# A fused transformer kernel: the high part of the rotated queries and keys is copied on GpSimd instead of ScalarE, and the order of the work is fitted anew

## The reference

```python
x = x + attn_a(layernorm(x), ...)
x = x + ffn(layernorm(x), w_gate, w_up, w_down)
x = x + attn_b(layernorm(x), Wqkv, Wout, bout)
x = x + ffn(layernorm(x), w_gate, w_up, w_down)

# in attn_b
re = te * cos - to * sin
ro = te * sin + to * cos
q_rot, k_rot = rotate(q), rotate(k)
num = exp(q_rot @ k_rot.T * scale)                  # rotated queries and keys
den = sum(exp(q @ k.T * scale), keys)               # not rotated, over all keys
attn = where(causal, num / den, 0)
y = attn @ v @ Wout + bout
```

## Time and profile before

| | before |
|---|---|
| median of 3 runs | 2028.87 us (2023.63 to 2030.54) |
| the profiled execution: its own time | 2020.54 us |
| its span, first to last instruction | 2018.3 us |
| TensorE busy | 1802.5 us, 89% |
| VectorE busy | 1429.3 us, 71% |
| ScalarE busy | 1429.0 us, 71% |
| GpSimd busy | 803.8 us, 40% |
| granted TensorE clock, mean | 0.946 |

### The profile page before, as it was taken

One profiled execution on the slowest core, in us unless ns is written; L12 is line 12 of the kernel. 1 busy time (PEld: TensorE's weight loads), 2 busy tenths in 40 slices (PEclk: granted clock), 3 DMA queues, 4 the chain that ended last, 5 costly groups with the idle time before them and its releaser, 6 DMA issues.

```text
span 2018.3 us, 63373 instructions
## 1 busy us (share of the span) xinstructions
PE 1802.5 (89%) x25221; PEld 1140.4 (57%) x25221; DVE 1429.3 (71%) x2978; ACT 1429.0 (71%) x3591; POOL 803.8 (40%) x1140
## 2 busy tenths in 40 slices
PE   5577999999899999999899999999999999998775
PEld 3363556566565655656565565656565565655444
DVE  6374768677686867768786877778786777865634
ACT  2227787786868778786877869686877868687590
POOL 0423343533434343443434344343435434344431
PEclk9687999999998999999999999999999999999897
DMA  5223344352524435253534525253443525243321
GB/s 155 64 56 90 87 129 98 100 119 77 136 63 131 91 101 124 78 130 69 137 78 116 122 76 127 72 134 70 138 100 89 127 75 139 61 125 90 73 68 36
DMA packets 129204, 199.51 MB, mean 99 GB/s; under 512 B 26720, under 2 KB 60512, under 8 KB 128880
## 3 DMA queue, kind: packets, MB, share of 16 engines
q1 hardware_dynamic: 128912, 195.44, 38.1%
HBM read 67.87 MB, written 51.52 MB: 59 GB/s over the span
## 4 chain that ended last, share of the span: by engine, by line
PE 47%; ACT 19%; DVE 16%; DMA 7%; issue 5%; SPq 3%; POOL 2%; POOLq 0%; DVEq 0%; ACTq 0%
PE psum L1120 14%; ACT psum L1236 7%; PE psum L1138 7%; ACT probs_B L1226 6%; PE psum L1150 5%; DMA xn<-o_scr_B 4%; PE psum L1017 4%; ACT probs_A L1219 3%; PE psum L1084 3%; PE psum L1094 3%; PE psum L1053 3%; DVE top L1410 2%; SPq L634 2%; PE psum L883 2%; PE psum L1038 2%
## 5 line engine op out<-in xcount | busy, mean ns | idle before, releaser
L1236 ACT ACTIVATE psum<-psum 128x512 f32<-128x512 f32 x1024 | 605.2, 598 | 164.4 <-PE psum L1017 163.5
L1659 POOL TENSOR_TENSOR h<-tmp,h 128x512 f16<-128x512 f32 x192 | 227.6, 1185 | 423.1 <-DVE h L1540 412.7
L1226 ACT ACTIVATE probs_B<-psum 128x512 f32<-128x512 f32 x640 | 334.5, 630 | 34.8 <-PE psum L1038 32.6
L1676 POOL TENSOR_SCALAR_AFFINE_SELECT probs_B<-probs_B 128x256 f32<-128x256 f32 x512 | 201.4, 421 | 117.7 <-ACT probs_B L1226 117.6
L1017 PE MATMUL psum<-pack_b 48*128 48x512 f16 x1024 | 176.9, 394 | 39.6 <-DMA pack_b<-src_b 20.3
L1120 PE MATMUL psum<-xT,w_u 128*128 128x256 f16 x1536 | 210.9, 278 | 1.2
L1120 PE MATMUL psum<-xT,w_g 128*128 128x256 f16 x1536 | 208.8, 280 | 3.1 <-ACT xT L1254 2.6
L1236 ACT ACTIVATION_READ_ACCUMULATOR psum<-psum 128x1 f32 x1024 | 204.2, 199 | 0.0
L1138 PE MATMUL psum<-w_d,h 128*128 128x256 bf16 x1536 | 194.7, 273 | 5.6 <-POOL h L1659 5.6
L1642 POOL TENSOR_TENSOR veps<-mv,eps 128x4 f32<-128x4 f32 x64 | 12.9, 202 | 426.0 <-DVE mv L1490 426.0
L1523 DVE SCALAR_TENSOR_TENSOR tmp<-tmp,psum 128x512 f32<-128x512 f32 x192 | 128.1, 680 | 69.9 <-ACT tmp L1265 69.3
(11 more groups left out here) (150 smaller groups left out, 3229.3 us busy)
## 6 DMA issues: line engine op xcount, KB each, us to landing
pack_b<-src_b SPq DMA_DIRECT2D x768, 64.0 KB, 2.4
pack_a<-src_a SPq DMA_DIRECT2D x384, 64.0 KB, 2.3
x<-in_L_attn_a_x_dram SPq DMA_DIRECT2D x32, 512.0 KB, 4.3
o_scr_A<-o_raw SPq DMA_DIRECT2D x64, 256.0 KB, 4.7
o_scr_B<-o_raw SPq DMA_DIRECT2D x64, 256.0 KB, 2.8
xn<-o_scr_A SPq DMA_DIRECT2D x32, 256.0 KB
rden_on<-r_scr_A SPq DMA_DIRECT2D x32, 256.0 KB
x_scr<-x SPq DMA_DIRECT2D x16, 512.0 KB, 3.1
```

Of the source, the lines that this page charges most:

```text
L1226: act.activation(probs["B"][:, i, :], score_bank("NP", n // 2, q, n % 2)[:, :], ACT.Exp, scale=SM_SCALE / W_SCALE ** 2)\
L1236: act.activation(bank[:, :], bank[:, :], ACT.Exp, scale=SM_SCALE / W_SCALE ** 2, accum_out=den[:, 0, j, 2 * tile + e, t:t + 1]).then_inc(d ...
L1659: pool.tensor_tensor(h[1][:, i % 2, :], tmp[:, i % 2, :], h[0][:, i % 2, :], ALU.subtract)\
L1676: ins = pool.affine_select(a, a, [[0, 2], [1, P]], ALU.is_ge, 0.0, base=0, channel_multiplier=-1)
```

## The change

The copy of the high part moves from ScalarE to GpSimd, where it stands between the sum and the difference of the same tile. GpSimd then waits only for itself inside a rotation (and, at tile 0, for the loads of the sequence before, as ScalarE did). ScalarE's step W2 is gone.

```diff
-            def rot_high_step(n, q):
-                if n == 0 and q:
-                    for packed in r_packed:
-                        act.wait_ge(packed, q * 96)
-                act.wait_ge(rot_sum, q * 4 + n + 1)
-                act.activation(src_b[:, 1, n // 2, 0, n % 2, :], tmp[:, n, :], ACT.Copy).then_inc(rot_high, 1)
...
-                elif kind == "W2":
-                    rot_high_step(n, q)
...
             def rotate(n, q):
                 pool.wait_ge(gu_taken, taken("W", n, "RB", q))
                 pool.tensor_tensor(tmp[:, n, :], tmp[:, n, :], turned[:, n % 2, :], ALU.add).then_inc(rot_sum, 1)
+                if n == 0 and q:
+                    for packed in r_packed:
+                        pool.wait_ge(packed, q * 96)
+                pool.wait_ge(rot_sum, q * 4 + n + 1)
+                pool.tensor_copy(src_b[:, 1, n // 2, 0, n % 2, :], tmp[:, n, :]).then_inc(rot_high, 1)
                 pool.wait_ge(rot_high, q * 4 + n + 1)
                 pool.tensor_tensor(src_b[:, 1, n // 2, 1, n % 2, :], tmp[:, n, :], src_b[:, 1, n // 2, 0, n % 2, :], ALU.subtract)\
                     .then_inc(rot_ready, 1)
```

Besides, nearly all places of `AT` are new. Here are the ones that the text below speaks of:

```diff
-    "MX": (435.36,),
+    "MX": (420.14,),
-    "TC": (518.06,),
+    "TC": (513.64,),
-    "AO": (585.97, 626.12, 670.95, 678.73),
+    "AO": (591.66, 631.81, 676.64, 684.42),
-    "UL": (1027.19, 1054.99, 1101.57, 1218.45),
-    "RL": (1056.62, 1109.32, 1128.13, 1277.55),
-    "VB": (1057.97, 1067.28),
+    "UL": (1026.26, 1055.94, 1101.57, 1218.45),
+    "RL": (1064.09, 1109.43, 1127.87, 1277.66),
+    "VB": (1054.67, 1058.09),
-    "W": (1031.74, 1039.53, 1050.63, 1054.55),
+    "W": (1024.4, 1031.88, 1050.77, 1054.93),
-    "OAOH": (788.67, 811.98),
+    "OAOH": (788.76, 807.16),
```

More of the change, by code:

```diff
@@ L64 @@
 AT = {
[37 rows of a table removed]
-    "VBC": (1064.43, 1086.91),
-    "VA": (362.08, 390.23),
-    "VAC": (363.66, 391.38),
[37 rows of a table added]
+    "VBC": (1063.61, 1089.48),
+    "VA": (362.62, 392.01),
+    "VAC": (364.2, 393.16),
     "GW": (419.32,),
     "GL": (435.68,),
-    "SL": (381.05, 382.82, 385.25, 385.26),
+    "SL": (376.13, 376.81, 378.36, 386.76),
     "GB": (361.17,),
-    "W": (1031.74, 1039.53, 1050.63, 1054.55),
[L110 to L120, removed]
-    "OAOH": (788.67, 811.98),
-    "OAOW": (811.19, 818.14),
-    "OAO": (834.24, 844.65),
-    "OAOX": (834.2, 843.29),
+    "W": (1024.4, 1031.88, 1050.77, 1054.93),
+    "W1": (1032.84, 1039.56, 1051.1, 1054.22),
+    "W2": (1046.09, 1047.49, 1066.55, 1074.59),
+    "PAT": (328.61, 335.99, 340, 341.74),
+    "PAT1": (326.11, 343, 348.59, 349.54),
+    "PAT2": (332.05, 345.78, 352.05, 353.11),
+    "PBT": (1021.34, 1022.28, 1023.29, 1030.79),
+    "PBT1": (1005.88, 1007.52, 1012.23, 1014.21),
+    "PBT2": (1017.3, 1022.87, 1022.96, 1033.41),
+    "OAOR": (773.75,),
+    "OAOL": (740.73, 742.65),
+    "OAOM": (784.47, 785.26),
+    "OAOH": (788.76, 807.16),
+    "OAOW": (813.57, 820.52),
+    "OAO": (835.66, 848.1),
+    "OAOX": (834.29, 845.41),
     "OBOR": (1445.53,),
@@ L128 @@
     "OBOH": (1469.95, 1493.14),
-    "OBOW": (1476.04, 1498.47),
+    "OBOW": (1476.04, 1497.64),
     "OBO": (1506.04, 1512.17),
     "OBOX": (1514.72, 1516.81),
-    "F2L0": (1518.94,),
-    "F2L1": (1519.78,),
+    "F2L0": (1519.1,),
+    "F2L1": (1527.26,),
     "F2L2": (1528.16,),
@@ L136 @@
     "F2L4": (1529.9,),
[L137 to L143, removed]
+    "F2L5": (1531.36,),
+    "F1L0": (855.74,),
+    "F1L1": (860.42,),
+    "F1L2": (874.74,),
+    "F1L3": (879.29,),
+    "F1L4": (879.42,),
+    "F1L5": (881.28,),
     "PBL0": (992.38,),
     "PBL1": (993.27,),
-    "PBL2": (1001.55,),
+    "PBL2": (998.26,),
     "PBL3": (1002.19,),
-    "PBL4": (1003.04,),
+    "PBL4": (1002.24,),
     "PBL5": (1003.44,),
@@ L155 @@
     "NAL5": (289.13,),
-    "PAX": (310.79,),
+    "PAX": (308.6,),
     "PAXH": (305.1,),
-    "PAX1": (310.5,),
-    "F2X": (1532.2,),
+    "PAX1": (310.6,),
+    "F2X": (1538.46,),
     "F2XH": (1529.11,),
[L161 to L176, removed]
-    "F2G": (1545.75, 1555.51, 1556.13, 1604.18, 1632.91, 1645.18),
-    "F2GT": (1546.01, 1559.36, 1563.11, 1604.39, 1636.03, 1637.16),
@@ L179 @@
[L179 to L184, removed]
+    "F2X1": (1535.52,),
+    "F1X": (893.37,),
+    "F1XH": (896.17,),
+    "F1X1": (898.23,),
@@ new lines @@
+    "PBX": (1005.33,),
+    "PBXH": (1004.99,),
+    "PBX1": (1009.1,),
+    "F1G": (905.82, 920.25, 920.77, 943.15, 944.81, 960.64),
+    "F1GT": (903.42, 922, 923.69, 938.76, 940.08, 962.09),
+    "F1U": (905.83, 922.19, 939.68, 944.8, 956.9, 961.69),
+    "F1H": (905.53, 922.18, 925.53, 947.43, 952.7, 962.34),
+    "F1I": (911.33, 926.9, 945.8, 948.36, 954.82, 967.6),
+    "F1J": (912.38, 929.16, 946.91, 949.89, 959.07, 968.69),
+    "F1JL": (906.14, 934.14, 952.99, 953.27, 955.88, 967.72),
@@ new lines @@
+    "F1FD": (921.55, 949.92, 953.37, 964.39, 975.08, 979.39),
+    "F1E": (954.1, 985.1),
+    "F2G": (1545.75, 1555.51, 1556.13, 1604.18, 1632.91, 1645.18),
+    "F2GT": (1546.01, 1561.04, 1563.11, 1604.39, 1636.03, 1639.07),
+    "F2U": (1546.58, 1583.59, 1593.26, 1614.82, 1652.18, 1666.45),
+    "F2H": (1550.35, 1565.49, 1573.89, 1612.12, 1639.65, 1653.71),
+    "F2I": (1550.55, 1585.28, 1604.9, 1617.89, 1656.06, 1665.06),
+    "F2J": (1561.02, 1589.92, 1608.32, 1637.95, 1658.78, 1742.83),
+    "F2JL": (1550.76, 1559.94, 1571.75, 1617.53, 1664.86, 1716.96),
@@ L185 @@
+    "F2FD": (1589.4, 1626.43, 1650.08, 1735.08, 1745.92, 1761.18),
     "F2E": (1665.78, 1763.07),
-    "XL": (717.21,),
-    "BI": (725.47,),
+    "XL": (716.12,),
+    "BI": (724.71,),
     "XS": (1775.82,),
```

## The result

The changed kernel takes 2034.62 us (median of 20 runs, 2027.11 us the lowest) beside 2026.33 us for the kernel before on the same chip (20 runs, 2021.48 to 2032.56): a ratio of 1.0043, with a 95% interval of 1.003 to 1.0057. One of the 20 executions took 6428.1 us and is left out of the ratio. I had forecast 2023 us and called faster the likeliest; it is 0.4% slower. The centre lies beyond the 0.3% that I had taken as the bound to no change, and the interval begins at it. The time lies inside my range of 2006 to 2043 us. The profiled execution took 2030.66 us (before: 2020.54 us), with a mean granted clock of 0.944.

A forecast was written before the change was run, and what follows sets the result against it. TensorE's work bounds most of a turn, SyncE's queue and two transfers the stretch from 972 to 991 us. ScalarE 0, rotation 0, OH 1 -4, first turn -2 sum to -6 us: 2023 us, range 2006 to 2043.

The forecast's parts named there:

- MX goes ahead of RL 3 on SyncE: SyncE's queue: RL 3's loads go behind MX but still land before NP 15 needs them; cost 0, 1.7 us cover.
- V 0 ahead of DP 0: TensorE, b's first products: V fills the 1.21 us gap, but the idling moves to O 0; gain 0.
- DP 9 ahead of X 0: TensorE's order: not priced singly, left among exchanges of neighbours on engines that stay busy either way.
- OH 1: VectorE's cast for OA, ahead of J 4, no longer meets GpSimd's work: 0.28 us a turn, 4 us gained, bounds 0 and 15.
- the cast: New fp32 to fp16 cast on GpSimd, 64 times: 0.61 us each, between bounds of 487 and 1187 ns.
- the rotations' chain: GpSimd's four serial rotations: 0.77 us replaces 0.83 us in each, so as long as before, 13 to 14 us; counted 0.
- what ScalarE gets back: ScalarE loses copies of 40.2 us, but their time turns into longer waiting for TensorE; counted 0.
- First turn: First turn with b: V fills part of TensorE's 3.36 us gap ahead of DP 0; 2 us gained.
- A: Filled idle time counts: the gap ahead of DP 0 and part of ScalarE's wait are won, 21 us, 2008 us; chance 0.16.
- B: No gain: VectorE's cast meets another GpSimd instruction, the first turn's gap is followed by ScalarE's load; 2029 us; chance 0.13.
- C: GpSimd's cast takes as long as the subtraction, rotations end 2.1 us later, NP 0 is late; 12 us, 2041 us; chance 0.11.
- D: Contention: GpSimd's new casts meet VectorE's casts, each 0.97 us longer; 15 us if on OM 1 or OH 1, 2043 us; chance 0.13.

The follow-up runs named there:

- e3_after_rl_first: The changed kernel with RL 3's loads back ahead of MX on SyncE; 2017.91 us, 0.9987 of the kernel before.
- e10_gl_first: The changed kernel with only GL 0, the load of the global tokens' values, moved ahead of RL 3, behind MX; 2015.48 us, 0.9979 of the kernel before.
- e6_v_back: e3_after_rl_first with W 3 back ahead of DP 0, V 0 behind DP 1 and V 1 behind DP 3; 2011.84 us, 0.9955 of the kernel before.
- e7_before_oh1: The kernel before with only OH 1 of OA put ahead of J 4 of F2 on VectorE; 2009.75 us, ratio 0.9948.
- e1_cast_only: The kernel before with the copy moved to GpSimd and all places as before; 2020.53 us, ratio 0.9996.
- e8_cast_oh1: e1_cast_only with OH 1 of OA put ahead of J 4 of F2; 2009.26 us, 0.9942 of the kernel before.
- e4_before_mx_first: The kernel before with RL 3 put behind MX on SyncE, and so GL 0 behind both; 2065.9 us, ratio 1.0228.

## Why the prediction was wrong

**The step that failed** is "MX goes ahead of RL 3 on SyncE [...] Cost 0, with 1.7 us of cover". What it says of RL 3 and NP 15 holds: RL 3's issues take 3.93 us (3.9 forecast), and NP 15 waits in no turn but the last. But it followed only the loads that moved back and not the one behind them. GL 0 stood behind MX before and behind MX and RL 3 after, its cover was about 1 us, and it came 2.3 us later. Taking it back is worth 0.56% as e3_after_rl_first (0.9987 for 1.0043), 0.64% as e10_gl_first (0.9979), ratios from different chips. Against my sum of -6 us this is a missing term of +11 to +13 us, and with it alone the sum would be +5 to +7 us; +8.3 us was measured.

**V 0 ahead of DP 0**, "The idle time moves from 979 to 987 us and nothing is gained: 0", was right in its mechanism and wrong in its price. The idling moved, but O 1 then ran partly at the lower clock in many turns (over 2.4 us in five of eleven here and in eight of e3_after_rl_first, 1.66 to 1.68 us in all of before), and e6_v_back gives 0.32% back (0.9955 for 0.9987; the intervals overlap, the traces show the mechanism). **DP 9 ahead of X 0** was among "the rest", which "exchanges neighbours on engines that stay busy either way". The exchange puts a step that waits 0.58 us for a bank ahead of the one that leads to the FFN; the timelines show it, the time leaves it at 0.16% and unsettled.

**OH 1** was the right mechanism, undersized: -0.28 us a turn was forecast, with 15 us as the bound of the whole. The stretch up to O 1 of a became 0.74 us a turn shorter, and e7_before_oh1 measures 0.52%, 10.5 us, where I had 4. The bound was worked out from the cast's 0.97 us and held; the value came from the idle figure of 0.28 us, which leaves out the pipeline's tail: six products last 0.98 us and twelve 1.66, so six more cost 0.68 us, and starts that are 1032.49 - 1031.23 = 1.26 us apart lose 0.58 us.

**Right by size:** the cast (0.61 us forecast, 0.61 undisturbed and 0.688 on the mean), GpSimd's and ScalarE's busy time (843 and 1389 us forecast, 842.6 and 1395.4 measured), the rotations' chain (13 to 14 us forecast; 13.6 us in the turn shown, 14.25 us on the mean), and 0 for what ScalarE gets back: e1_cast_only is at 0.9996. ScalarE's idle time before the row sums grew by 43.2 us. **First turn:** TensorE's gap ahead of DP 0 there shrank from 3.36 to 1.67 us in the changed kernel. What that was worth was not tried by itself, so the 2 us stay open.

**Rivals.** A (filled idle time counts) is contradicted by e6_v_back, which leaves the gap ahead of DP 0 open and is the faster by its median and its turn. B (VectorE's cast meets another instruction instead) is refuted by e7_before_oh1: the cast is quick and the gain is there. C (a slow cast) and D (new meetings of casts) are refuted by e1_cast_only, and by e8_cast_oh1, which is as fast as e7_before_oh1. In the changed kernel too, OM 1, OH 1 and OW 1 of OB together take 2.48 us on the mean for 2.56 us before. The time came out where I had put C and D, for another reason. The loss that decided, a transfer queued behind the moved ones, was none of the rivals.

**The sum after the fact,** of ratios to the kernel before: cast -0.04%, OH 1 -0.52%, GL 0 +0.56%, V and W +0.32%, X 0 +0.16%: +0.48% for +0.43% measured. Each term carries an interval of about 0.15 to 0.3% to either side, so the agreement is closer than these runs can promise; the terms for GL 0 and OH 1 are the ones that stand well clear of it.

## What to carry to other kernels

When an issue is moved in a queue, list all that stands behind it until the queue next idles, and for each the distance from its issue to its first use; a load that nothing waits for today may have 1 us of cover. Idle time that is hidden behind a transfer is no reserve: filling it early can move the gap to the place where the engine's next work is on the path. And read a stall on TensorE from start to start of the products, with the spacing of undisturbed ones taken off, not from the idle figure alone.

## What the runs showed of the hardware

- v_glob's load (136 KB, one issue of 0.57 us) isn't there until 6.2 to 6.8 us after its issue began, in the middle turns of the changed kernel and of e4_before_mx_first alike (to the start of the product that waits for it; the last of its packets ends 5.6 to 6.3 us after the issue), while the 64 KB loads of pack_b have a median of 2.4 us from issue to landing.
- VectorE's cast of on_part has a median of 935 ns in the kernel before and of 428 ns in e7_before_oh1, where one exchange in VectorE's order keeps one of its four casts a sequence away from GpSimd's subtraction. The Trainium skill (GPSIMD Engine Reference, Key points) says that GpSimd shares its SBUF interfaces with VectorE and contends with VectorE's instructions in a two-port mode or with two inputs in SBUF; the trace agrees: the cast takes 1.38 us beside the subtraction and 0.42 us without it.
- GpSimd's cast, 0.61 us undisturbed, reaches 1.17 us at its slowest, and its sums range from 1.27 to 1.70 us in the rotation shown. It costs nothing that shows here: e1_cast_only is at 0.9996.
